# First pieces of the matrix in finer transfers and steps, and one step of a unit of h to each piece, in a one-core GNN layer

## The reference, cut to what matters

```python
h = jnp.maximum(_layernorm(x, axis=-1), 0.0)          # x is 8192 x 128
x = x + (1.0 - 0.1) * (adj @ h) + 0.1 * L0_gnn_h      # adj is 8192 x 8192, float32
```

## Time and profile before

| | before |
|---|---|
| median of 3 runs | 710.65 us (710.53 to 710.77) |
| the profiled execution | 710.53 us |
| its span in the profile | 708.4 us |
| TensorE busy | 703.5 us, 99% |
| VectorE busy | 634.5 us, 90% |
| ScalarE busy | 531.8 us, 75% |
| DMA | 285.74 MB, mean 403 GB/s |

### The profile page before, as it was taken

How to read it: one execution, slowest core, us unless ns; L and a number is a source line. 1 busy time by engine, 2 the same in 40 slices (tenths; PEclk the granted TensorE clock), 3 DMA queues, 4 the chain that set the end, 5 groups by cost and what they waited for, 6 DMA issues and landing times.

```text
span 708.4 us, 8165 instructions
## 1 busy us (share of the span) xinstructions
PE 703.5 (99%) x3086; PEld 577.8 (82%) x3086; DVE 634.5 (90%) x549; ACT 531.8 (75%) x463; POOL 26.8 (4%) x38
## 2 busy tenths in 40 slices
PE   9999999999999999999999999999999999999998
PEld 5878888888888888888888888888888888888886
DVE  4999999999999999999898888888988898889885
ACT  4899998788788787887776767676767676767673
POOL 1100000000000000000000000000000000000000
PEclk9999999999999999999999999999999999999999
DMA  9999999999999999999999999999999999999990
GB/s 364 419 418 418 419 419 416 419 418 416 421 415 418 420 417 419 417 417 422 417 402 415 407 412 384 382 399 412 413 421 405 423 420 422 421 421 422 414 412 20
DMA packets 46550, 285.74 MB, mean 403 GB/s; under 512 B 5168, under 2 KB 9520, under 8 KB 14000
## 3 DMA queue, kind: packets, MB, share of 16 engines
q1 hardware_dynamic: 46080, 283.99, 97.8%
q10 hardware_dynamic: 432, 1.25, 0.5%
HBM read 281.02 MB, written 4.19 MB: 403 GB/s over the span
## 4 chain that ended last, share of the span: by engine, by line
PE 94%; DMA 3%; DVE 1%; ACT 1%; SPq 0%; issue 0%; DVEq 0%
PE acc L457 16%; PE acc L453 16%; PE acc L452 16%; PE acc L436 15%; PE acc L441 15%; PE acc L430 15%; DMA raw<-wide_dram 3%; DVE a_lo L345 1%; ACT a_hi L301 0%; SPq L213 0%; SPq L196 0%; DVE stats L311 0%; ACT h_full L271 0%; DVE mean_var L321 0%; SPq L226 0%
## 5 line engine op out<-in xcount | busy, mean ns | idle before, releaser
L345 DVE TENSOR_TENSOR a_lo<-raw,a_hi 128x2048 fp32r<-128x2048 f32 (+1 forms) x292 | 582.4, 2010 | 58.1 <-ACT a_hi L301 57.1
L301 ACT ACTIVATE a_hi<-raw 128x2048 fp32r<-128x2048 f32 (+1 forms) x368 | 497.9, 1382 | 160.6 <-PE acc L457 100.1
L452 PE MATMUL acc<-a_hi,h_hi 128*128 128x512 f32 x512 | 199.2, 389 | 0.0
L453 PE MATMUL acc<-a_hi,h_lo 128*128 128x512 f32 x512 | 199.2, 389 | 0.0
L430 PE MATMUL acc<-a_hi,h_hi 128*128 128x512 f32 x504 | 167.9, 390 | 0.0
L436 PE MATMUL acc<-a_hi,h_lo 128*128 128x512 f32 x504 | 167.6, 389 | 0.1
L457 PE MATMUL acc<-a_lo,h_hi 128*128 128x512 f32 x512 | 136.8, 389 | 0.0
L441 PE MATMUL acc<-a_lo,h_hi 128*128 128x512 f32 x504 | 135.2, 389 | 0.1
L453 PEld LDWEIGHTS acc<-a_hi,h_lo 128*128 128x128 f32 x512 | 96.1, 188 | 20.0
L457 PEld LDWEIGHTS acc<-a_lo,h_hi 128*128 128x128 f32 x512 | 96.1, 188 | 19.9
L452 PEld LDWEIGHTS acc<-a_hi,h_hi 128*128 128x128 f32 x512 | 96.1, 188 | 19.9
(11 more groups left out here) (15 smaller groups left out, 30.5 us busy)
## 6 DMA issues: line engine op xcount, KB each, us to landing
raw<-tall_dram SPq DMA_DIRECT2D x128, 1024.0 KB, 8.3
raw<-wide_dram SPq DMA_DIRECT2D x126, 1024.0 KB, 11.1
res_sb<-res_dram SPq DMA_DIRECT2D x16, 512.0 KB, 9.9
x_sb<-x_dram SPq DMA_DIRECT2D x30, 128.0 KB, 11.1
out_dram<-finished SPq DMA_DIRECT2D x15, 256.0 KB, 8.5
raw<-early_dram ACTq DMA_DIRECT2D x2, 512.0 KB, 6.7
raw<-early_dram SPq DMA_DIRECT2D x2, 512.0 KB, 5.9
out_dram<-finished SPq DMA_DIRECT2D x2, 128.0 KB, 1.8
```

The source lines that it names most:

```text
L301: nc.scalar.activation(a_hi[:, q % SPLIT_SLOTS, cols], raw[:, q % RAW_SLOTS, cols], ACT.Copy).then_inc(hi_ready, 1)
L345: nc.vector.tensor_tensor(a_lo[:, q % SPLIT_SLOTS, cols], raw[:, q % RAW_SLOTS, cols], a_hi[:, q % SPLIT_SLOTS, cols].bitcast(fp32), ALU.s ...
L452: nc.tensor.matmul(bank, h_hi[:, k, :], a_hi[:, slot, cols], start=(k == 0), stop=False)
L453: nc.tensor.matmul(bank, h_lo[:, k, :], a_hi[:, slot, cols], start=False, stop=False)
```

## The change

Five edits. Piece 0 comes in four parts of 128 x 512 instead of two of 128 x 1024; parts 0 and 2 are issued by SP, 1 and 3 by ACT (before: part 0 by SP, 1 by ACT). Piece 1 stays in two parts. The a_lo of pieces 2 to 9 is made in four steps of a quarter instead of two of a half. The steps of a unit go to other pieces: before, for the units up to block 15, x was loaded at due-5, statistics and aggregation stood behind piece due-5, the shift behind due-4 (later units: x at due-6, one block's statistics behind due-6 and the other's behind due-5); now for all units x is loaded at due-5, both statistics stand behind due-6, the aggregation behind due-4, the shift behind due-3, and scale (due-2) and h_hi and h_lo (due-1) stay. WARM_UP is 21 instead of 22. Seven fewer lines make the numbers of the changed file 7 lower from there on.

```diff
-PARTS = {_q: 2 for _q in range(EARLY)}
+PARTS = {0: 4, 1: 2}
...
-BY_SCALAR = [(0, 1), (1, 1)]
+FINE_LOW = range(NATIVE, 10)
+
+BY_SCALAR = [(0, 1), (0, 3), (1, 1)]
...
-LATE = 16
...
-    if _a < LATE:
-        LOAD_X_AT[_due - 5] = _u
-        STATS_AT[_due - 5] = [_a, _a + 1]
-        AGGREGATE_AT[_due - 5] = SHIFT_AT[_due - 4] = _u + 1
-        SCALE_AT[_due - 2] = _u
-    else:
-        LOAD_X_AT[_due - 6] = _u
-        STATS_AT[_due - 6] = STATS_AT.get(_due - 6, []) + [_a]
-        STATS_AT[_due - 5] = [_a + 1]
-        AGGREGATE_AT[_due - 5] = SHIFT_AT[_due - 4] = _u + 1
-        SCALE_AT[_due - 2] = _u
-    HIGH_H_AT[_due - 1] = _u
+    LOAD_X_AT[_due - 5] = _u
+    STATS_AT[_due - 6] = [_a, _a + 1]
+    AGGREGATE_AT[_due - 4] = SHIFT_AT[_due - 3] = _u + 1
+    SCALE_AT[_due - 2] = HIGH_H_AT[_due - 1] = _u
...
-WARM_UP = 22
+WARM_UP = 21
...
-    if q in FINE and halves is PARTS:
+    if q in FINE and halves is PARTS or q in FINE_LOW:
         return [1, 2, 3, 4]
...
-        part_landed = [[sem(f"part_landed{s}_{i}") for i in range(2)] for s in range(RAW_SLOTS)]
+        part_landed = [[sem(f"part_landed{s}_{i}") for i in range(4)] for s in range(RAW_SLOTS)]
```

## The result

The changed kernel takes 712.39 us (median of 7 runs, 711.64 to 713.90); the kernel before, measured along with it, 710.36 (7 runs, 710.15 to 710.77). The ratio is 1.0031 with an interval of 1.0021 to 1.0040: slower by 0.31%, 2.03 us, where a gain of 0.10% was forecast. The profiled execution took 712.40 us, its span 710.6.

What follows compares the result with a forecast made beforehand. TensorE was taken as the bound, never waiting from piece 13 on. Piece 13 moving from 43.82 to 43.05 gave 0.77, less 0.03 for smaller packets, 0.74 us: median 710.65 to 709.9, range 709.2 to 710.8.

Steps and rivals of the forecast that it cites:

- Same instructions, other pieces: Moving the steps of units other than unit 2 was taken to cost nothing.
- draws ahead: After piece 13, DVE was to need 10.4 us for four pieces against TensorE's 10.88.
- third rival: ACT waits for a late shift, with DVE behind ACT; at 0.1 us a unit, 712.9 us; chance 0.05.
- The second term: Smaller transfers of piece 0 at the start were to cost 0.03 us, between 0 and 0.1.
- that rival: The gain is hidden by later landings or thin DVE margins at pieces 12 and 13: under 0.4 us; chance 0.21.
- The give-back: At pieces 9 to 11 TensorE was to lose its earlier gains by waiting for the same landings.
- the 0.34 at piece 4: TensorE's third a_lo product waits for DVE at piece 4; a_lo in quarters was to end this 0.34 us stall.
- the 0.57: At piece 12 TensorE loses 0.57 us waiting for h_lo, then a_lo; moved unit steps were to end both waits.
- The gains add up: Rival: pieces 9 to 11 land sooner and all three gains count, 1.56 us, or 709.1; chance 0.12.
- The start: The first real product was to start at 5.52 instead of 6.17, 0.65 us sooner, given back at pieces 9 to 11.
- 43.05: Forecast start of piece 13 on TensorE in us, instead of 43.82.
- from piece 13 on TensorE never waits: From 43.82 us on TensorE takes 2.72 us a piece without waits, so all gains must lie before.

Runs made afterwards that it cites:

- e2: Kernel before with only piece 0 in quarters by turns and 21 warm-up products: 711.61 us, ratio 1.0019.
- e3_fine_low: Kernel before with only the a_lo of pieces 2 to 9 in four steps: 709.95 us, ratio 0.9995.
- e1_tables: Kernel before with only the new places of a unit's steps: 711.88 us, ratio 1.0021.
- b2_best_fine14: t3_agg_after_h_lo with a_lo in four steps from piece 2 up to piece 13: 709.27 us, ratio 0.9988.
- t3_agg_after_h_lo: e1_tables with the aggregation back at due-5 and h_lo made ahead of it, shift still at due-3: 709.84 us, ratio 0.9993.
- e4: The changed kernel with the old places of a unit's steps: 710.86 us, ratio 1.0008.
- f1: As e2, but each quarter of piece 0 lies without gaps in a block of its own in HBM: 711.46 us, ratio 1.0016.
- g1: Kernel before, each half of piece 0 in two transfers of 64 partitions with 4 KB rows: 714.24 us, ratio 1.0055.
- f2_no_turns: As e2, but SP issues quarters 0 and 1 and ACT 2 and 3: 712.36 us, ratio 1.0030.

## Why the prediction was wrong

**The step that failed.** For the other units the prediction said "Same instructions, other pieces", and of DVE that it "draws ahead" at 10.4 us for four pieces against TensorE's 10.88. The wait for `rstd` stood in that sum at nothing, without a reason; the runs show 0.59 us a unit, and 1.96 us of TensorE by piece 128. The instructions are the same, but what runs beside them isn't. The changed kernel's DVE around the unit due at piece 100, from one aggregation to the next:

```profile
272.13 0.24 DVE L314 BATCH_NORM_AGGREGATE mean_var<-stats 128x2 f32<-128x6 f32 x2
272.40 0.17 DVE L317 TENSOR_SCALAR var_eps<-mean_var 128x2 f32<-128x2 f32 x1
272.49 2.29 DVE L338 TENSOR_TENSOR a_lo<-raw,a_hi 128x2048 fp32r<-128x2048 f32 x1
275.37 0.16 DVE L323 SCALAR_TENSOR_TENSOR shift<-mean_var,rstd 128x2 f32<-128x2 f32 x1 [0.59 <-POOL rstd L257]
275.45 2.29 DVE L338 TENSOR_TENSOR a_lo<-raw,a_hi 128x2048 fp32r<-128x2048 f32 x1
277.66 0.48 DVE L304 BATCH_NORM_STATS2 stats<-x_sb 128x6 f32<-128x128 f32 x2
278.28 2.29 DVE L338 TENSOR_TENSOR a_lo<-raw,a_hi 128x2048 fp32r<-128x2048 f32 x1
280.49 0.42 DVE L330 TENSOR_TENSOR h_lo<-h_full,h_hi 128x256 fp32r<-128x256 f32 x1
280.82 2.29 DVE L338 TENSOR_TENSOR a_lo<-raw,a_hi 128x2048 fp32r<-128x2048 f32 x1
283.03 0.24 DVE L314 BATCH_NORM_AGGREGATE mean_var<-stats 128x2 f32<-128x6 f32 x2
```

GpSimd beside it:

```profile
272.65 2.68 POOL L257 TENSOR_TENSOR rstd<-var_eps,exponent 128x2 f32<-128x2 f32 x1 [8.83 <-DVE var_eps L317]
283.55 2.68 POOL L257 TENSOR_TENSOR rstd<-var_eps,exponent 128x2 f32<-128x2 f32 x1 [8.22 <-DVE var_eps L317]
```

And ACT:

```profile
275.56 0.88 ACT L264 ACTIVATE h_full<-x_sb,shift,rstd 128x128 f32<-128x128 f32 x2 [3.10 <-DVE shift L323]
276.35 1.90 ACT L294 ACTIVATE a_hi<-raw 128x2048 fp32r<-128x2048 f32 x1
```

`rstd` is released when var_eps is done, at 272.57. DVE is by then on the next a_lo, which ends at 272.49 + 2.29 = 274.78, and `rstd` ends at 275.33, 0.55 later. DVE stands 0.59 at the shift. The four pieces take from 272.13 to 283.03, 10.90 us: 10.3 of work and the 0.59. ACT waits for the shift too, with a_hi behind it, which ends at 278.25; the next a_lo starts at 278.28, so no slack is left there either. TensorE needs 10.88 for four pieces, so DVE never gains on it, and each residual sum (L346, 0.6 of DVE's time, one in ten pieces) is lost for good; the prediction's 10.4 left that out too. GpSimd's `rstd` starts at 205.71 and, twelve units later, at 338.99: 11.11 a unit, 2.7 us behind TensorE's pace over the twelve. DVE's lead takes the first part of it, TensorE's waits the rest.

Why 20 times: the a_lo is one whole step from piece 40 on, and 21 units are aggregated behind piece 40 or a later one. With halves the same `rstd` takes 1.61 us and is done inside the 2.36 of the two, so the units before have no wait. One of the 21 escapes: there DVE had to wait for ACT's a_hi, and `rstd` was at work before the a_lo started. GpSimd's row and DVE's:

```profile
128.38 0.70 POOL L257 TENSOR_TENSOR rstd<-var_eps,exponent 128x2 f32<-128x2 f32 x1 [8.22 <-DVE var_eps L317]
128.64 2.29 DVE L338 TENSOR_TENSOR a_lo<-raw,a_hi 128x2048 fp32r<-128x2048 f32 x1 [0.34 <-ACT a_hi L294]
```

So 0.70 us is what `rstd` takes with DVE idle at its start. Otherwise its length follows the DVE instruction that stands behind var_eps:

| behind var_eps, on DVE | it ends at | `rstd` takes | ends at | later by |
|---|---|---|---|---|
| h_lo, 0.42 (before, 29.05) | 29.47 | 0.80 | 30.01 | 0.54 |
| quarter of a_lo (after, 22.03) | 22.72 | 1.08 | 23.28 | 0.56 |
| half of a_lo (after, 43.47) | 44.69 | 1.61 | 45.24 | 0.55 |
| whole a_lo, 2.29 (after, 272.49) | 274.78 | 2.68 | 275.33 | 0.55 |

In each, `rstd` ends about 0.55 us behind the end of that instruction, as if most of its 0.70 could begin only then. That the two share a port is inferred from this. The Trainium skill, "SBUF — State Buffer", section "SBUF: two separate sides", says it outright: DVE and GpSimd share a port pair under an exclusive lock, and a DVE operation with two SBUF inputs holds it for the whole instruction against a GpSimd one that reads SBUF. a_lo and h_lo both have two inputs, so this case's rows agree: 0.80, 1.08, 1.61 and 2.68 us for one and the same GpSimd instruction. The section also says that whichever of the two starts first blocks the other fully. The case with GpSimd first shows no block here: the a_lo at 128.64 started while `rstd` was at work and took its usual 2.29.

The sign was there to read before the change. In the kernel before, unit 1's `rstd` had a half of a_lo behind var_eps, unit 2's had h_lo; GpSimd's timeline:

```profile
18.89 1.60 POOL L264 TENSOR_TENSOR rstd<-var_eps,exponent 128x2 f32<-128x2 f32 x1 [11.35 <-DVE var_eps L324]
29.21 0.80 POOL L264 TENSOR_TENSOR rstd<-var_eps,exponent 128x2 f32<-128x2 f32 x1 [8.72 <-DVE var_eps L324]
```

Two durations of one instruction, with its place as the only difference, and the prediction never priced `rstd` at its new place. Its third rival, "ACT waits for the shift", named the direction, the waiting engines and the shape of the loss, and gave it 0.05, because the 100 us of ACT's waits on TensorE spoke against it. Those lie in the tall pieces, where no h is made; they were no evidence for the wide ones. The trigger was another than the rival's, though: it had DVE late, and not `rstd`.

**The second term was mis-sized.** "I take 0.03 us, between 0 and 0.1" for smaller transfers: alone the quarters cost 1.35 us (e2), and piece 2's a_hi starts at 13.30 instead of 11.47 in the changed kernel. The rate of 432 GB/s with halves said nothing of quarters. The remark that issue is covered by a DMA share of 1.00 held in e2 (1.02), but a busy share isn't a rate: 333 GB/s at 1.02 against 417 at 1.03. The Trainium skill's "DMA: Bandwidth & Descriptors", section "Bandwidth", had spoken against it, with 1 MB or more wanted, in a table for transfers issued from GpSimd; the prediction worked out 0.6 us from it and gave that rival 0.21. The direction was the page's; the size here was twice that, and halves of 0.5 MB show nothing of it.

**The give-back didn't happen.** The prediction had TensorE lose at pieces 9 to 11, by waiting for the same landings, whatever it gained before, the 0.34 at piece 4 included. In no kernel of the table does any of these pieces take TensorE more than 2.74 us. From the start of piece 2 to that of piece 13 it takes 31.11 us in the kernel before, 30.70 in e3_fine_low, where the wait at piece 4 is gone, and 30.17 in e1_tables and b2_best_fine14, where the one at piece 12 is gone too: 0.94 less, so the 0.34 and the 0.57 add up. The pieces also land sooner: ACT starts a_hi of piece 10 at 33.12 in t3_agg_after_h_lo and at 33.28 in b2, against 33.54. For these two terms the rival "The gains add up", with its 0.12, was right.

**What held.** With quarters the first product waits for h_full and no longer for the transfer, as forecast. That it started at 5.13 and not at 5.5 is chance: x landed sooner in this execution, and h_full was ready at 5.08 instead of 5.47; in e2 and e4, with the same quarters, the product starts at 5.82 and 5.86. The start was worth nothing at the end. a_lo in quarters ended the wait at piece 4, and its 0.14 a piece of DVE's time (2.50 for four steps, 2.36 for two) cost TensorE nothing; e3 gives -0.31, within its interval of nothing. The wait at piece 12 went by the mechanism described. That e1 has piece 13 at 43.07, where 43.05 was forecast, is luck: the forecast took no gain at piece 4 and got there by landings, while e1 has that gain and a piece 2 that starts 0.18 later (12.90). And "from piece 13 on TensorE never waits, and nothing that the change does there can make it faster" was true, but it hid the other half: things there could make it slower.

**Open.** Why small transfers at the head of both queues slow the transfers is not settled. Rows, place in HBM and turns are ruled out as the whole cause. In f1 the DMA engines idle (share 0.82 from 4 to 6 us, 267 GB/s), in e2 they are busy at 295 GB/s over the same stretch; one explanation should cover both, and none that was tried does.

## What to carry to other kernels

When an instruction is moved, look at what stands behind and beside it on the other engine at the new place, and read whether the same instruction already has two durations in the trace; a count by line that stays equal while its mean can move hides this. An engine with spare time on average still becomes the bound if a wait inside its period brings the period to that of the engine ahead. Where a steady stretch has a margin of a few tenths of a microsecond per period, add up the period of the engine that feeds it, with every extra step and wait in it, before calling a move free.

## What the hardware showed that was not expected

- GpSimd's 128x2 power takes 0.70 us with DVE idle at its start and up to 2.68 us by the DVE instruction beside it (table above).
- 256 KB transfers at the head of both queues: 308 to 333 GB/s from 4 to 8 us in five kernels, against 413 to 426 with 512 KB ones in seven. The 256 KB transfers to 64 partitions (g1): 227.
- In f2_no_turns TensorE waited 1.98 us for a part, and then its granted clock fell. Windows (same columns as above):

```profile
8.00:10.00 2.00, 1.74 (x3) 0.72 (x4) 0.15 (x1) 1.72 (x4) 0.00 (x0) 0.62 1.04 432
10.00:12.00 2.00, 2.00 (x4) 0.93 (x3) 0.55 (x1) 0.00 (x0) 0.00 (x0) 0.52 1.01 416
```

Its weight loads, each behind one fp32 pass:

```profile
8.25 0.31 PEld L416 LDWEIGHTS acc<-raw,h_full 128*128 128x128 f32 x2 [1.98 <-DMA raw<-early_dram]
9.07 0.34 PEld L416 LDWEIGHTS acc<-raw,h_full 128*128 128x128 f32 x1 [0.51 <-issue]
9.93 0.34 PEld L416 LDWEIGHTS acc<-raw,h_full 128*128 128x128 f32 x1 [0.52 <-issue]
```

The passes lie 0.86 us apart at a clock near 0.5, which is the level of 1.2 GHz; in the changed kernel they lie 0.43 apart at a clock of 1.00, 2.4 GHz. In the changed kernel waits of 1.45 and 1.92 us left the clock at 1.00.
